# Second layer norm of eight token tiles: from iterations 4 to 11 of an attention loop to its four draining iterations

## What is computed

```python
# x (16, 64, 512), ctx (16, 512, 512)
x = x + cross_attention(layernorm(x), ctx)   # scores, the 32 largest kept, softmax, @ v, @ Wo
x = x + wave_field(layernorm(x))             # q, k, v, gate; deposit k_feat * v, convolution along tokens, @ Wout
x = x + ffn(layernorm(x))                    # ternary weights, gelu
def layernorm(x):
    return (x - mean(x)) / sqrt(var(x) + 1e-5)
```

## Time and profile before

| | us |
|---|---|
| median of 3 runs (lowest, highest) | 502.63 (502.43, 503.21) |
| span of the profiled execution | 499.2 |
| attention loop, its first transposes to ACT's cast of wgq | about 84 to 246 |
| of that, iterations 8 to 11 (draining) | about 209 to 246 |
| busy in the span: PE, DVE, ACT, POOL | 462.3, 328.8, 242.2, 239.9 |

### The profile page before, as it was taken

One profiled execution on the slowest core, in us unless ns is written; L12 is line 12 of the kernel. 1 busy time (PEld: TensorE's weight loads), 2 busy tenths in 40 slices (PEclk: granted clock), 3 DMA queues, 4 the chain that ended last, 5 costly groups with the idle time before them and its releaser, 6 DMA issues.

```text
span 499.2 us, 6243 instructions
## 1 busy us (share of the span) xinstructions
PE 462.3 (93%) x2172; PEld 365.9 (73%) x2172; DVE 328.8 (66%) x585; ACT 242.2 (49%) x385; POOL 239.9 (48%) x267
## 2 busy tenths in 40 slices
PE   6949999868999999989959999999998999999996
PEld 2436875647888887768748888888786888888885
DVE  0859999869799999995476579464675323252333
ACT  1258983847678787765423444643345111121211
POOL 2530909567689777782260068133433673323230
PEclk9978999979899999999989999999999999999999
DMA  6994072052344333243000030000000000020002
GB/s 230 402 405 166 0 252 86 6 164 85 105 149 135 120 119 136 84 164 131 1 0 1 1 106 1 21 1 0 1 1 0 1 0 0 1 85 1 1 0 84
DMA packets 19998, 40.54 MB, mean 81 GB/s; under 512 B 1920, under 2 KB 1920, under 8 KB 19456
## 3 DMA queue, kind: packets, MB, share of 16 engines
q1 hardware_dynamic: 19968, 40.16, 22.9%
HBM read 38.05 MB, written 2.10 MB: 80 GB/s over the span
## 4 chain that ended last, share of the span: by engine, by line
PE 50%; DVE 27%; ACT 8%; POOL 5%; issue 5%; DMA 3%; SPq 1%; DVEq 0%; ACTq 0%
PE bank L1460 6%; PE bank L1461 5%; PE bank L1476 5%; PE bank L1474 5%; PE bank L1099 5%; PE bank L1101 5%; PE bank L1100 5%; POOL nat_lo L377 3%; PE bank L1152 3%; DMA ctxr<-ctx 2%; PE bank L1246 2%; DVE mt_lo L898 2%; DVE ln_s L737 2%; DVE xn L999 2%; PE bank L1106 2%
## 5 line engine op out<-in xcount | busy, mean ns | idle before, releaser
L377 POOL TENSOR_TENSOR nat_lo<-ctxr,nat_hi 128x512 fp32r<-128x512 f32 x64 | 83.8, 1336 | 20.1 <-ACT nat_hi L571 19.7
L712 ACT ACTIVATE g<-bank,b1c 128x512 f32<-128x512 f32 x32 | 22.1, 690 | 88.9 <-PE bank L1476 88.9
L1079 DVE CAST g_hi<-g 128x512 fp32r<-128x512 f32 x32 | 13.7, 427 | 74.6 <-ACT g L712 74.5
L1460 PE MATMUL bank<-w2s,g_lo 128*128 128x512 f32 x128 | 50.0, 390 | 1.8 <-DVE g_lo L1081 1.8
L439 POOL TENSOR_SCALAR w2s<-w2t 128x512 fp32r<-128x512 int8 x32 | 19.8, 620 | 66.0 <-PE bank L1461 66.0
L1474 PE MATMUL bank<-xt_lo,w1s 128*128 128x512 f32 x128 | 50.0, 391 | 0.0
L1476 PE MATMUL bank<-xt_hi,w1s 128*128 128x512 f32 x128 | 49.8, 389 | 0.0
L1461 PE MATMUL bank<-w2s,g_hi 128*128 128x512 f32 x128 | 49.8, 389 | 0.0
L549 ACT ACTIVATE mt_hi<-bank 128x512 fp32r<-128x512 f32 x64 | 37.5, 596 | 20.8 <-PE bank L1246 20.5
L898 DVE TENSOR_TENSOR mt_lo<-bank,mt_hi 128x512 fp32r<-128x512 f32 x64 | 43.4, 683 | 6.1 <-ACT mt_hi L549 5.8
L1246 PE MATMUL bank<-ident,ctxr 128*128 128x128 f32 x256 | 40.5, 285 | 6.6 <-DMA ctxr<-ctx 6.5
(11 more groups left out here) (232 smaller groups left out, 1217.0 us busy)
## 6 DMA issues: line engine op xcount, KB each, us to landing
ctxr<-ctx SPq DMA_DIRECT2D x32, 512.0 KB, 3.5
w1raw<-w1T SPq DMA_DIRECT2D x1, 4096.0 KB, 21.9
w2raw<-w2T SPq DMA_DIRECT2D x1, 4096.0 KB, 29.4
wgraw<-wgT SPq DMA_DIRECT2D x4, 1024.0 KB, 5.1
resid<-x SPq DMA_DIRECT2D x2, 1024.0 KB, 9.0
out<-resid SPq DMA_DIRECT2D x8, 256.0 KB, 2.2
wqraw<-wq SPq DMA_DIRECT2D x4, 256.0 KB, 3.7
wkraw<-wk SPq DMA_DIRECT2D x4, 256.0 KB, 4.8
```

Source lines behind the costliest of these rows:

```text
L377: pool.tensor_tensor(nat_lo[:, par, c, :], ctxr[:, b % 4, c, :], f(nat_hi[:, par, c, :]), ALU.subtract).then_inc(nat_lo_ok, 1)
L1460: pe.matmul(to, g_lo[:, n % 2, token(k)], w2s[:, n % 2, :], start=(c == 0), stop=False)
```

## The change

All eight tiles of the second layer norm move to iterations 8 to 11: tile 0 in iteration 8, tiles 1 and 2 in 9, 3 and 4 in 10, 5, 6 and 7 in 11 (`late_tiles`). On PE the transposes of the first tile of iterations 8, 9 and 10 (0, 1, 3) stand right behind the first quarter of `project` and ahead of `weigh`; tile 2 and 4 stand later in their iterations, tile 5 between `k_product(1)` and `v_product(0)`, tiles 6 and 7 behind `v_product(0)`. The banks are 0 and 1 for tiles 0 to 2 and 4 and 5 for the others, both halves of `xn` are used, and `turn_prob` no longer waits for `xt_lo_ok`. `k_product(0)` waits for the xt_lo of tile 2 also, whose bank it takes. (Blank lines are left out.)

```diff
@@ -236,6 +236,14 @@
             return 4 + t if t < 4 else t - 2
+        def late_tiles(i):
+            return ((0,), (1, 2), (3, 4), (5, 6, 7))[i - NT] if i >= NT else ()
+        def late_bank(t):
+            return bank[t % 2 if t < 3 else 4 + t % 2]
         def first_xn(t):
             return xn6[:, t, :] if t < NT - 2 else xn[:, t - NT + 2, :]
@@ -393,8 +401,8 @@
                         pool.affine_select(out=k, in_=k, compare_op=ALU.is_ge, fill=0.0, base=0,
                                            pattern=[[0, H], [1, T]], channel_multiplier=-1).then_inc(kern_cut, 1)
                     pool.wait_ge(kern_cut, 3)
-                if 0 <= i - 4 < NT:
-                    rstd(NT + i - 4)
+                for t in late_tiles(i):
+                    rstd(NT + t)
                 nat_lo_part(i - 1, 0)
                 split_q(i + 1, 0)
                 nat_lo_part(i - 1, 1)
@@ -539,6 +547,16 @@
                 act.activation(hi, wgraw[:, n, :, :], ACT.Copy).then_inc(wg_hi_ok[n], 1)
+            def late_apply(t):
+                if t >= 2:
+                    act.wait_ge(xn_turned, NT + t - 1)
+                ln_apply(NT + t, t, xn[:, t % 2, :])
+            def late_xt(t):
+                xt_part(NT + t, t, late_bank(t))
             for i in range(NT + 4):
                 def mt_hi_part(j):
                     g = 2 * DC * i + j
@@ -591,13 +609,26 @@
                                    ACT.Copy).then_inc(at_hi_ok, 1)
                 mt_hi_part(1)
                 cross(i - 1, 1)
+                if i == NT:
+                    late_apply(0)
+                if i == NT + 1:
+                    late_apply(1)
+                    late_apply(2)
+                    late_xt(1)
+                if i == NT + 2:
+                    late_apply(3)
+                    late_apply(4)
+                    late_xt(3)
+                    late_xt(4)
+                if i == NT + 3:
+                    late_apply(5)
+                    late_apply(6)
+                    late_xt(5)
+                    late_apply(7)
+                    late_xt(6)
+                    late_xt(7)
                 mt_hi_part(2)
                 mt_hi_part(3)
-                p = i - 4
-                if 0 <= p < NT:
-                    if p:
-                        act.wait_ge(xn_turned, NT + p)
-                    ln_apply(NT + p, p, xn[:, 0, :])
                 nat_hi_part(i - 1, 0, (0, 1))
                 p = i - 1
                 if 0 <= p < NT:
@@ -605,6 +636,8 @@
                     if p:
                         act.wait_ge(prob_turned, p)
                     act.activation(prob[:, :], s_t[:, :], ACT.Exp, bias=nmax[:, :], scale=SCALE).then_inc(exp_ok, 1)
+                if i == NT:
+                    late_xt(0)
                 mt_hi_part(4)
                 am_part(i - 2, 0)
                 if i == NT + 1:
@@ -615,9 +648,8 @@
                 nat_hi_part(i - 1, 1, (0, 1))
                 mt_hi_part(6)
                 am_part(i - 2, 1)
-                p = i - 4
-                if 0 <= p < NT:
-                    xt_part(NT + p, p, bank[4])
+                if i == NT + 1:
+                    late_xt(2)
                 mt_hi_part(7)
                 nat_hi_part(i - 1, 1, (2, 3))
                 p = i - 2
@@ -890,6 +922,10 @@
                 dve.tensor_tensor(lo, raw, f(hi), ALU.subtract).then_inc(wg_lo_ok[n], 1)
+            def late_xt(t):
+                xt_lo_part(NT + t, t, late_bank(t))
             for i in range(NT + 4):
                 def mt_lo_part(j):
                     g = 2 * DC * i + j
@@ -926,11 +962,17 @@
                     dve.tensor_tensor(at[:, :, :, T:P], bank[4][:, :].rearrange("p (c b n) -> p b c n", c=SC, b=2),
                                       f(at[:, :, :, 0:T]), ALU.subtract).then_inc(at_lo_ok, 1)
                 mt_lo_part(1)
-                if 0 <= i - 4 < NT:
-                    dve.wait_ge(x1_ok, i - 3)
-                    layer_stats(NT + i - 4, i - 4)
+                for t in late_tiles(i):
+                    dve.wait_ge(x1_ok, t + 1)
+                    layer_stats(NT + t, t)
+                if i == NT + 1:
+                    late_xt(1)
                 if i == NT + 2:
                     split_lo(1, wv_lo[:, :, :], wgraw[:, 1, :, :], wv_hi[:, :, :])
+                    late_xt(3)
+                if i == NT + 3:
+                    for t in late_tiles(i):
+                        late_xt(t)
                 sum_rows(i - 1, 1)
                 mt_lo_part(2)
                 if 0 <= i - 1 < NT:
@@ -953,8 +995,10 @@
                 if i == NT + 1:
                     dve.wait_ge(am_ps, B)
                     split_lo(0, wk_lo[:, :, :], wgraw[:, 0, :, :], wk_hi[:, :, :])
-                if 0 <= i - 4 < NT:
-                    xt_lo_part(NT + i - 4, i - 4, bank[4])
+                if i == NT:
+                    late_xt(0)
+                if i == NT + 1:
+                    late_xt(2)
                 mt_lo_part(7)
                 p = i - 3
                 if 0 <= p < NT:
@@ -1211,6 +1257,7 @@
                 pe.wait_ge(xt_lo_ok, NT + t + 1)
                 if t == 0:
                     pe.wait_ge(scores_ok, 2 * NT)
+                    pe.wait_ge(xt_lo_ok, NT + 3)
                 if t >= 2:
                     pe.wait_ge(kb_ok, t - 1)
                 for d in range(DC):
@@ -1231,6 +1278,19 @@
+            def late_turn(t):
+                pe.wait_ge(ln_ready, NT + t + 1)
+                if t < 2:
+                    pe.wait_ge(mt_lo_ok, 4 * B)
+                elif t == 2:
+                    pe.wait_ge(xt_lo_ok, NT + 1)
+                elif t < 5:
+                    pe.wait_ge(am_ok, B)
+                else:
+                    pe.wait_ge(xt_lo_ok, NT + t - 1)
+                turn(late_bank(t), xn[:, t % 2, :]).then_inc(xn_turned, 1)
             for i in range(NT + 4):
                 def chunk(j):
@@ -1308,8 +1368,6 @@
                         pe.wait_ge(kept_ok, pair + 1)
                         if pair >= 1:
                             pe.wait_ge(am_ok, 2 * pair - 1)
-                        if pair >= 3:
-                            pe.wait_ge(xt_lo_ok, NT + pair - 2)
                         turn(bank[4], prob).then_inc(prob_turned, 1)
                 g0 = 2 * DC * i
@@ -1317,7 +1375,10 @@
                 if i >= NT + 2:
                     k_product(i - NT - 2)
                 if i == NT + 3:
+                    late_turn(5)
                     v_product(0)
+                    late_turn(6)
+                    late_turn(7)
                 chunk(0)
                 if i == 2:
                     score(g0 - 3)
@@ -1327,6 +1388,8 @@
                 if i == 2:
                     turn_prob(0)
                 project(i - 3, (0,))
+                if NT <= i < NT + 3:
+                    late_turn(late_tiles(i)[0])
                 chunk(2)
                 score(g0 + 2 - ahead)
                 weigh(i - 2, 0, 0)
@@ -1343,15 +1406,14 @@
                 score(g0 + 5 - ahead)
                 weigh(i - 2, 1, 1)
                 join(i - 2, 0)
-                if 0 <= i - 4 < NT:
-                    pe.wait_ge(ln_ready, NT + i - 4 + 1)
-                    if i - 2 < NT:
-                        pe.wait_ge(am_ok, 2 * (i - 2) + 1)
-                    turn(bank[4], xn[:, 0, :]).then_inc(xn_turned, 1)
+                if i == NT + 1:
+                    late_turn(2)
                 chunk(6)
                 score(g0 + 6 - ahead)
                 if i != NT + 2:
                     project(i - 3, (2, 3))
+                else:
+                    late_turn(4)
                 chunk(7)
                 score(g0 + 7 - ahead)
                 join(i - 2, 1)
```

## The result

| us | before | after |
|---|---|---|
| median of four runs each on one chip (lowest, highest) | 502.92 (502.43, 503.32) | 514.14 (513.67, 516.0) |
| ratio of after to before, 95% interval | | 1.0258 (1.0211 to 1.0306) |
| span of the profiled execution | 499.2 | 511.9 |
| the same kernel again on another chip: median, ratio, span | 501.65 | 513.57, 1.0241 (1.0208 to 1.0275), 512.1 |

The account below looks back on a forecast made before the run. PE and DVE were both taken as full in iterations 4 to 7, with PE room in the drain. Loop - 2.75, standstills + 3.0, clock + 2.4 and tail + 4.1 gave + 6.75 us: 509.4 us, range 504.5 to 512.5.

Parts of the forecast that it names:

- who waits for the delayed products: Iteration 8: ACT's amsb and second half of nat_hi wait, then POOL, whose eight nat_lo end only 0.3 us later.
- Loop: Iterations 4 to 7, one layer norm tile removed from each: 2.31 us by iteration 7 plus 0.44, a 2.75 us gain.
- the turn of 15.94 us: Loop turns fall from 16.71 us to iteration 3's 15.94, PE's pace replacing DVE's: 0.77 us won a turn.
- this loop and its ends: Context buffers, nat_lo to DMA to PE transpose: gain 1.1 us if every DMA takes 4.6, 3.75 if the last takes 3.5.
- A to J at full clock: From DVE's amt_lo of pair 5 (A) to pair 7's first join (J), iterations 8 and 9: 3.0 us later.
- The clock in iterations 8 and 9: A low-clock stretch after each of two PE standstills of about 3 us: 1.2 us charged twice, 2.4; ends 0 and 3.4.
- the rival in which the clock holds: Both standstills leave PE at 2.4 GHz: + 4.35 us, 507.0 us; chance 0.17.
- J to S: Tail, from pair 7's first join (J) to ACT's cast of wgq (S): 4.1 us later; price between 0 and 5.8.
- the step called covered: Iteration 10 or 11: tile 4 meets DVE's split of wv, slowing POOL, but PE's projection covers it; nothing added.
- S to end: From ACT's cast of wgq (S) to the end: all as before, 0 us.
- The rival in which that idle hides the tail: The 4.1 us vanish in PE's 5.15 us idle; with 3.75 gain and a holding clock, - 0.75, 501.9 us; chance 0.10.
- The rival with more low stretches: Full clock price twice, a third low stretch in iteration 11, loop gain 1.1: + 11.1, up to 513.7 us; chance 0.16.

Follow-up runs that it names:

- e5: After with tile 0's transposes in iteration 8 moved behind the first half of weigh, still ahead of the second: 508.97 us, ratio 1.0150.
- e7: After without the context loads of batches 8 to 15 (buffers keep those of 4 to 7, output differs): 511.95 us, ratio 1.0214.
- e10: After with eight added matmuls, results unused, ahead of tile 5's transposes in iteration 11: 513.49 us, ratio 1.0249.
- the spread ones: After with statistics of tiles 1 to 5 in iteration 9, 6 in 10, 7 in 11, transposes behind other products: 500.84 us; e9_spread_turns is the second.
- e9_spread_turns: Against the spread kernel of 500.84 us: tile 6's transposes ahead of k_product(1), tile 7's ahead of v_product(0); 498.34 us, ratio 0.9947.

## Why the prediction was too low

The step that failed in mechanism is the one on who waits for the delayed products: the prediction let POOL's nat_lo end 0.3 us late, and at full clock they came 2.7 us late. The other misses are terms that had the wrong size: the loop's turn, the length of the low stretches, and the tail.

**Loop, -2.75 predicted, -2.01 measured.** The step that failed here is the turn of 15.94 us. After's turns take (192.25 - 143.65)/3 = 16.20 us, so 0.51 is won in each and not 0.77; the last piece gave 0.47 against 0.44. The 15.94 was a turn that only PE limits, which the kernel without loads confirms (16.0), but in after the context buffers limit too. PE waits 0.19 and 1.03 us for them, and the chain of iterations 5 to 7 runs over DMAs of 3.52 and 4.03 us and the nat_lo between. The prediction had this loop and its ends, 1.1 and 3.75 us of gain; the run without loads gave 3.8, and the ten other profiles with this loop, measured as here, 1.6 to 2.4. The mean of the two ends was nearer than the row chosen.

**A to J at full clock, +3.0 predicted, +5.4 measured** (25.24 - 19.86). This is the error of mechanism. The prediction moved all 19 products by 3.1 us and then named as ACT's waiting work only amsb and the second half of nat_hi, so POOL would end 0.3 us late. But it is the first nat_hi that waits, and a queue that starts late ends late: 2.7 us at full clock, 2.4 more than said. That is the whole miss of this term (3.0 + 2.4 = 5.4). In before and in both kernels that free it, nat_hi comes straight behind ACT's xn of tile 0; the change puts eight products between the two. The 19.86 holds before's own low stretch, and the chain over POOL that sets J in after does not pass it. The standstill in iteration 8 was right (3.16 for about 3); the one in iteration 9 was 4.07, since POOL came late; with tile 0 moved back it was 3.53.

**The clock in iterations 8 and 9, +2.4 predicted, +3.2 measured.** The mechanism was right, and the rival in which the clock holds is refuted. 0.51 and 0.50 over about 3.5 us cost nearly the full price of 1.7 each; the 1.2 counted on a low stretch of 3.4 us that is partly over before the work starts. The second did begin inside the wait, but it was twice as long (226.1 to 232.8 us) and still covered 3.4 us of work. The Trainium skill, page "TensorE: Matmul & The Clock Gate", section "Why this matters for your kernels", warns of idle gaps; these two rows agree, the third place above agrees four times in seven. The row at 223 us, which the prediction called in agreement, came behind three idles of at most 1.09 us, and the single idles of 1.00 and 1.03 us in iteration 7, in before and in after, were followed by no low stretch; it bears less on that warning of the Trainium skill than the prediction said.

**J to S, +4.1 predicted, +6.15 measured.** At full clock, as in three profiles (e5, e7, e10), it is 21.2 - 16.64 = 4.6; the low stretch is the other 1.6, which the sum left out and a rival had. The 0.5 at full clock is the step called covered; that is read off the trace, no run tests it. ln_rs of tile 4 (POOL, then ACT and DVE):

```profile
242.97 2.52 POOL L350 TENSOR_TENSOR ln_rs<-ln_ve,neg_half 128x1 f32<-128x1 f32 x1
...
245.95 0.82 ACT L467 ACTIVATE xn<-resid,ln_nb,ln_rs 128x512 f32<-128x512 f32 x1 [2.17 <-POOL ln_nb L352]
246.67 0.58 ACT L473 ACTIVATE xt_hi<-bank 128x512 fp32r<-128x512 f32 x1
...
242.80 2.28 DVE L922 TENSOR_TENSOR wv_lo<-wgraw,wv_hi 128x2048 fp32r<-128x2048 f32 x1
...
247.28 0.69 DVE L778 TENSOR_TENSOR xt_lo<-bank,xt_hi 128x512 fp32r<-128x512 f32 x1 [2.20 <-ACT xt_hi L473]
247.89 0.74 DVE L1008 SCALAR_TENSOR_TENSOR resid<-bank,rinv,resid 128x512 f32<-128x512 f32 x1
```

It took 2.52 us and not 0.55, beside DVE's split of wv. PE had cover for that. ACT had not: its program puts xn of tile 4 ahead of xt_hi of tile 3, whose xt_lo stands ahead of resid of tile 7 on DVE. resid comes at J + 12.04 us, in e5 and e10 too, in before at 11.48 (241.13 - 229.65). The Trainium skill, page "SBUF — State Buffer", section "Who interferes with whom", has the lock; the row agrees, and the prediction followed its cost on one engine only.

**S to end, 0 predicted, +0.35 measured**, and PE's idle for k_raw 5.22 for 5.15. In the nine other profiles but the spread ones this part takes 252.7 to 253.5 us, so the 0.35 is within what executions differ by. The rival in which that idle hides the tail is refuted: the idle hangs on the cast and moved with it.

Together: 0.7 of the loop, -0.4 ahead of it, 2.4 of nat_hi, 0.8 of the clock in 8 and 9, 0.5 of ln_rs, 1.6 of the third low stretch and 0.35 at the end are the 5.95 us that were missing by spans. By the medians 4.5 us were missing (11.2 against 6.75), for the reason given under the table of parts. The rival with more low stretches (+11.1) came nearest, with its three stretches and its tail (5.8 for 6.15). Its number is in part luck: its loop gain was too small by 0.9 us and its A to J by 2.2, and the two offset each other in part.

## What to carry over

When a wait is put ahead of ready work on an in-order engine, list the consumers of the first instruction behind it as well as of the last, engine by engine: the buffer that the first one frees may start the longest queue, here eight subtractions of 1.3 us. Moving the same transposes behind that work kept the loop's gain and gave back what the waits had cost, 4.2 and 5.2 us for one call each on PE. Price a standstill with the slow clock behind it (1.6 us for each standstill of 3 to 4 us in after), since whoever waits for the work behind it pays too. And when a run lands on the expected time, check part by part that the time moved where the theory said: in the kernel without loads two other parts moved by more than 1 us each.

## What the hardware showed that was not expected

- The same idle of 1.96 us, at the same place in the program, was followed by a low stretch in four profiles and by none in three. In before, three idles of 0.44, 1.09 and 0.60 us were followed by one; in the kernel with tiles 0 and 1 back and the v product first, idles of 0.39, 0.29 and 1.39 us at the same place were not.
- From 40 us on, the low stretches of all thirteen profiles are about 3.4, 6.8 or 10.2 us long. Behind the same standstill of 3.16 us one lasted 3.4 us in after and 6.8 us without the loads. How much low clock comes differs between executions of one kernel, and the time goes with it: of the twelve runs of e9_spread_turns the fastest (497.6 us) has a mean granted clock of 0.983, the slowest (501.1 us) 0.972.
- The lock hit ln_rs harder in after than ln_nb in before (1.82 us in place of 0.26): 2.52 us in place of 0.55, in all twelve profiles that are not before's. In the spread kernels it is that of tile 6.
- Eleven profiles of the same loop code (all but before and the kernel without loads) took 63.4 to 64.2 us from the third chunk of iteration 4 to A. One profile fixes a loop's pace to about 0.4 us, not better.
